# Ten record bodies instead of seven scattered after the attention's gathers, in a graph network kernel on one Trainium2 core

## The reference, cut to what matters

```python
edge_index = jnp.stack([src, dst])
x = x + attention(layernorm(x), edge_index)          # softmax over each node's edges, sum of att * h[dst]
x = x + token_ffn(layernorm(x))                      # router, top half of the tokens, 256 -> 1024 -> 256
x = x + gcn(layernorm(x), edge_index, type, attr)    # three layers over all edges
x = x + experts(layernorm(x))                        # two of 8 experts
...
ew = edge_attr @ edge_w + edge_b                     # inside gcn
msg = relu(x[src] * ew)
h_i = segment_sum(msg * (type == i), dst)            # for each of 3 types, then @ weights[l, i]
```

## Time and profile before

| | |
|---|---|
| three runs | 6016.11, 6029.7 and 6051.34 us, median 6029.7 us |
| the profiled execution | 6056.04 us, of it span 6054.2 us |
| busy in the span | PE 4511.0 us (75%), DVE 4198.5 (69%), POOL 4119.8 (68%), ACT 2286.1 (38%) |
| granted TensorE clock, mean | 0.895 |
| last sort step until the first gather of the attention | 1026 to 1114 us: PE busy 1.01 us, DVE 6.85, POOL 66.69 |
| attention | 1114 to 2181 us: PE busy 914.42 us, DVE 759.92, ACT 598.23, POOL 816.71 |
| token network | 2181 to 2414 us |
| three message layers | 2437 to 5780 us: POOL busy 819.51, 818.14 and 818.19 us in them |

### The profile page before, as it was taken

One profiled execution on the slowest core, in us unless ns is written; L12 is line 12 of the kernel. 1 busy time (PEld: TensorE's weight loads), 2 busy tenths in 40 slices (PEclk: granted clock), 3 DMA queues, 4 the chain that ended last, 5 costly groups with the idle time before them and its releaser, 6 DMA issues.

```text
span 6054.2 us, 89560 instructions
## 1 busy us (share of the span) xinstructions
PE 4511.0 (75%) x25082; PEld 2816.0 (47%) x25082; DVE 4198.5 (69%) x9658; ACT 2286.1 (38%) x5880; POOL 4119.8 (68%) x4199
## 2 busy tenths in 40 slices
PE   6469986488888879677777767777777677777787
PEld 2135543366666646344444434444444344444455
DVE  8889986377777773676666657767676677777734
ACT  0039875355555532333333323333332232323321
POOL 1467777777777774777777757777776777777700
PEclk9579998688888879899899989999999899999989
DMA  5011110234333321544444434444444444444400
GB/s 147 19 39 29 26 27 22 72 105 109 107 101 101 102 57 39 164 135 135 128 130 130 132 104 138 137 139 138 139 139 121 133 139 138 139 138 139 138 29 21
DMA packets 445004, 624.93 MB, mean 103 GB/s; under 512 B 97098, under 2 KB 330260, under 8 KB 444563
## 3 DMA queue, kind: packets, MB, share of 16 engines
q0 software_dynamic: 187648, 457.52, 27.2%
q1 hardware_dynamic: 250164, 159.14, 9.3%
q10 hardware_dynamic: 6754, 2.96, 0.2%
HBM read 556.32 MB, written 62.94 MB: 102 GB/s over the span
## 4 chain that ended last, share of the span: by engine, by line
PE 27%; DVE 15%; issue 10%; POOL 6%; ACT 2%; DVEq 2%; DMA 2%; SPq 0%; POOLq 0%; ACTq 0%
PE banks L1169 13%; DVE acc_mem L1688 6%; POOL sort_mem L619 6%; DVE z_mem L1831 5%; PE banks L1199 4%; PE banks L1112 3%; PE banks L1102 3%; DMA sort_mem<-x_d,x_mem 2%; PE banks L1157 2%; DVEq L1677 1%; DVEq L1688 1%; ACT z_mem L805 1%; PE banks L1154 1%; ACT x_mem L816 1%; PE banks L1189 1%
## 5 line engine op out<-in xcount | busy, mean ns | idle before, releaser
L619 POOL DMA_INDIRECT sort_mem<-x_d,x_mem x2568 | 2461.9, 959 | 953.1 <-issue 831.5
L1169 PE MATMUL banks<-z_mem 128*128 128x257 f32 x5136 | 1579.8, 432 | 907.0 <-DVE acc_mem L1688 773.1
L1169 PEld LDWEIGHTS banks<-z_mem 128*128 128x128 f32 x5136 | 858.1, 200 | 1605.7 <-ACT z_mem L805 717.6
L1688 DVE TENSOR_TENSOR acc_mem<-acc_mem,banks 128x257 f32 x2568 | 1080.2, 421 | 565.2 <-PE banks L1169 391.2
L805 ACT ACTIVATE z_mem<-z_mem 128x512 f32<-128x512 f32 x1284 | 768.8, 628 | 1381.1 <-DVE z_mem L1831 1381.1
L1831 DVE TENSOR_TENSOR z_mem<-banks,sort_mem 128x512 f32<-128x512 f32 x1284 | 825.1, 685 | 411.9 <-PE banks L1157 292.8
L577 POOL DMA_INDIRECT recB_d<-acc_mem,sort_mem x740 | 787.8, 1065 | 428.1 <-issue 223.0
L586 POOL DMA_INDIRECT acc_mem<-h_d,xnt_mem x808 | 803.6, 995 | 246.3 <-issue 230.2
L1045 PE MATMUL banks<-acc_mem,xnt_mem 128*128 128x257 f32 x1616 | 577.3, 484 | 43.3 <-DVE acc_mem L1631 42.2
L1631 DVE SCALAR_TENSOR_TENSOR acc_mem<-acc_mem,z_mem,banks 128x257 f32 x808 | 386.4, 478 | 115.5 <-PE banks L1045 98.8
L1157 PE MATMUL banks<-z_mem,x_mem 32*128 32x256 f32 x5136 | 422.6, 405 | 0.0
(11 more groups left out here) (347 smaller groups left out, 5663.9 us busy)
## 6 DMA issues: line engine op xcount, KB each, us to landing
x_mem<-recB_d SPq DMA_DIRECT2D x642, 68.0 KB
sort_mem<-x_d,x_mem POOLq DMA_INDIRECT x2568
x_mem<-at_d SPq DMA_DIRECT2D x428, 64.0 KB
at_d<-x_mem SPq DMA_DIRECT2D x214, 64.0 KB
acc_mem<-h_d,xnt_mem POOLq DMA_INDIRECT x808, 2.8
x_mem<-x_d SPq DMA_DIRECT2D x100, 128.0 KB, 2.7
acc_mem<-in_edge_attr SPq DMA_DIRECT2D x40, 312.5 KB
recB_d<-acc_mem,sort_mem POOLq DMA_INDIRECT x740, 2.2
```

The costliest lines, as they stand in the source:

```text
L619: pool.indirect_dma_start(out=xg[h % XG][:, k, :], out_offset=None, in_=x_ds[l % 2], in_offset=bass.IndirectOffsetOnAxis(ap=reci[h][:, k, ...
L1169: m.matmul(bank[5 + tile % 2][:, :AC], oneh[:, Q % 2, k, :], msg[:, Q % 2, k, :], start=True, stop=True)\
L1688: v.tensor_tensor(a_, a_, bank_[:, :AC], ALU.add).then_inc(flushed, 1)
```

## The change

`SCATTERED_FIRST` becomes 30, and a new name, `RANKED_BESIDE`, keeps the old 33 for all that concerns the ranks: late ranks, their bank, their steps and the steps at which records are made stay as they were. So bodies 30, 31 and 32 are ranked and their records made as before, but POOL scatters them after the attention's gathers. The four slots of the ring then hold bodies 30 to 33, and bodies 34 to 39 need a slot each: four lie in the sort's memory, which is laid out anew so that what sort A alone needs stands together, one in `z_mem`, one in a new tensor. Room for that comes from `winpA`, packed window numbers that nothing read, and its four DVE instructions go. The products of the router's weights move to `acc_mem` (`tok_dots`), and a small memset of DVE moves behind the wait for the scatters.

```diff
-SCATTERED_FIRST = RANKED_FIRST + PAIRS // 4
+RANKED_BESIDE = RANKED_FIRST + PAIRS // 4
+SCATTERED_FIRST = RANKED_BESIDE - 3
...
-        late_recs = [sort_mem[:, a:a + 20 * RW].rearrange("p (c w) -> p c w", w=RW) for a in (EC, EC + 20 * RW, 5 * EC)]
+        late_mem = [sort_mem[:, 7 * EC // 2 + k * 20 * RW:7 * EC // 2 + (k + 1) * 20 * RW] for k in range(4)]
+        late_mem += [z(1650, 20 * RW), sb("late_rec", [P, 20 * RW])]
+        late_recs = [m_.rearrange("p (c w) -> p c w", w=RW) for m_ in late_mem]
...
-            return bank[4 + g % 2 if g < 4 * SCATTERED_FIRST else 7][:EP, :5 * BKT_B]
+            return bank[4 + g % 2 if g < 4 * RANKED_BESIDE else 7][:EP, :5 * BKT_B]
...
-            return 3 + 3 * (g - 4 * SCATTERED_FIRST)
+            return 3 + 3 * (g - 4 * RANKED_BESIDE)
...
-                if i >= 4:
-                    act.wait_ge(S(f"edges_put{i % 4}"), i // 4 * 320 if i < SCATTERED_FIRST + 4 else (i - 4) // 4 * 320)
+                if 4 <= i < SCATTERED_FIRST + 4:
+                    act.wait_ge(S(f"edges_put{i % 4}"), i // 4 * 320)
...
-                for i in range(SCATTERED_FIRST, BODIES):
+                for i in range(RANKED_BESIDE, BODIES):
                     if s_ == record_step(i):
                         make_records(i)
...
-                st.did(v.scalar_tensor_tensor(s["winp"], four[:, :, 1], 128.0, four[:, :, 0], ALU.mult, ALU.add))
...
-                st.run(v.tensor_tensor(dots, xn[:, t0:t0 + 5, :], vecs[:, 0:1, :].broadcast_to([P, 5, D]), ALU.mult))
-                st.run(v.tensor_reduce(tok_w[:, t0:t0 + 5], dots, X_AXIS, ALU.add))
+                st.run(v.tensor_tensor(tok_dots, xn[:, t0:t0 + 5, :], vecs[:, 0:1, :].broadcast_to([P, 5, D]), ALU.mult))
+                st.run(v.tensor_reduce(tok_w[:, t0:t0 + 5], tok_dots, X_AXIS, ALU.add))
...
-            st.did(v.memset(msg[:, :, :, D:AC], 1.0))
             for u in range(4):
                 dve.wait_ge(S(f"edges_put{u}"), BODIES // 4 * 320)
+            st.did(v.memset(msg[:, :, :, D:AC], 1.0))
```

More of the change, by code:

```diff
@@ L144, in build @@
         sort_mem = sb("sort_mem", [P, 7 * EC])
[L145 to L150, removed]
+        keyB = sort_mem[:EP, 0:EC // 2].bitcast(BF16)
+        itemB = sort_mem[:EP, EC // 2:5 * EC // 2].rearrange("p (c e) -> p c e", c=2)
+        addrB = sort_mem[:, 5 * EC // 2:7 * EC // 2].bitcast(INT32)
+        keyA = sort_mem[:EP, 7 * EC // 2:4 * EC].bitcast(BF16)
+        dstm, segp, tileA = (sort_mem[:EP, (4 + k) * EC:(5 + k) * EC] for k in range(3))
+        winpB = sb("winpB", [1, TB // 4], INT32)
         ordp = sb("ordp", [1, 4 * NT], INT32)
@@ L264, in build @@
         xt = xt_mem[:, 0:2 * NP_].rearrange("p (k n) -> p k n", k=2)
+        tok_dots = acc_mem[:, 0:5 * D].rearrange("p (t d) -> p t d", d=D)
         tok_w = small[:, 330:355]
@@ L308, in build @@
         baseB_d, baseA_d = dram("baseB_d", [3, EC * BKT_B], BF16), dram("baseA_d", [3, EC * BKT_A], BF16)
-        SORT_B = dict(nb=BKT_B, T=TB, cols=5, bodies=EC // 20, key=keyB, base_d=baseB_d, winp=winpB, n=0)
-        SORT_A = dict(nb=BKT_A, T=TA, cols=10, bodies=EC // 40, key=keyA, base_d=baseA_d, winp=winpA, n=1)
+        SORT_B = dict(nb=BKT_B, T=TB, cols=5, bodies=EC // 20, key=keyB, base_d=baseB_d, n=0)
+        SORT_A = dict(nb=BKT_A, T=TA, cols=10, bodies=EC // 40, key=keyA, base_d=baseA_d, n=1)
         GROUPS_B, GROUPS_A = EC // 5, EC // 10
@@ L323, in late_bank @@
         def late_bank(g):
-            return bank[4 + g % 2 if g < 4 * SCATTERED_FIRST else 7][:EP, :5 * BKT_B]
+            return bank[4 + g % 2 if g < 4 * RANKED_BESIDE else 7][:EP, :5 * BKT_B]
         def record_slot(i):
             return erec[:, i % 4, :, :] if i < SCATTERED_FIRST + 4 else late_recs[i - SCATTERED_FIRST - 4]
-        assert BODIES - SCATTERED_FIRST <= 7
+        assert BODIES - SCATTERED_FIRST <= 4 + len(late_recs)
         def late_step(g):
-            return 3 + 3 * (g - 4 * SCATTERED_FIRST)
+            return 3 + 3 * (g - 4 * RANKED_BESIDE)
         def record_step(i):
-            return 5 + 10 * (i - SCATTERED_FIRST)
+            return 5 + 10 * (i - RANKED_BESIDE)
         block = ctx.enter_context(nc.Block())
@@ L560, in _ @@
             g.memset(tri_b, 1.0).then_inc(S("p_const"), 1)
-            pool.wait_ge(S("p_const"), 15)
+            pool.wait_ge(S("p_const"), 12 + len(late_recs))
             g.memset(pick[:, 79:80], 1.0).then_inc(S("p_const"), 1)
@@ L565, in _ @@
                    base=0, channel_multiplier=24).then_inc(S("p_const"), 1)
-            pool.wait_ge(S("p_const"), 18)
+            pool.wait_ge(S("p_const"), 15 + len(late_recs))
             pool.sem_inc(S("fill_ready"), 1)
@@ L654, in make_records @@
                 a.activation(rec_[:, :, W_SEG], itemB[:, 1, i * 20:(i + 1) * 20], ACT.Copy).then_inc(S("attr_hi"), 1)
-            act.wait_ge(S("p_const"), 17)
+            act.wait_ge(S("p_const"), 14 + len(late_recs))
             act.wait_ge(S("items_ready"), 1)
@@ L928, in rank_late @@
                 pe.wait_ge(S("onehot2"), g + 1)
-                if g >= 4 * SCATTERED_FIRST:
+                if g >= 4 * RANKED_BESIDE:
                     pe.wait_ge(S("maskedB"), g)
@@ L1067, in _ @@
                         sum_rows(s_ - 2, k)
-                for g in range(4 * SCATTERED_FIRST, 4 * BODIES):
+                for g in range(4 * RANKED_BESIDE, 4 * BODIES):
                     if s_ == late_step(g):
@@ L1239, in _ @@
             st = Steps(dve, "dve_step")
-            dve.wait_ge(S("p_const"), 17)
+            dve.wait_ge(S("p_const"), 14 + len(late_recs))
             st.did(v.tensor_scalar(ident, iota, iota_col, None, ALU.is_equal))
@@ L1352, in count @@
                 st.run(v.tensor_scalar(w[:, 512:T], bank[6][:, :T - 512], float(nb), None, ALU.min))
-                four = w[0:1, :T].rearrange("p (a b) -> p a b", b=4)
-                upper = winge[0:1, :T // 4].bitcast(INT32)
-                st.did(v.scalar_tensor_tensor(s["winp"], four[:, :, 1], 128.0, four[:, :, 0], ALU.mult, ALU.add))
-                st.run(v.scalar_tensor_tensor(upper, four[:, :, 3], 128.0, four[:, :, 2], ALU.mult, ALU.add))
-                st.run(v.tensor_single_scalar(upper, upper, 14, ALU.logical_shift_left))
-                st.run(v.tensor_tensor(s["winp"], s["winp"], upper, ALU.bitwise_or))
-                if n_ == 0:
+                if n_ == 0:
+                    four = w[0:1, :T].rearrange("p (a b) -> p a b", b=4)
+                    upper = winge[0:1, :T // 4].bitcast(INT32)
+                    st.did(v.scalar_tensor_tensor(winpB, four[:, :, 1], 128.0, four[:, :, 0], ALU.mult, ALU.add))
+                    st.run(v.scalar_tensor_tensor(upper, four[:, :, 3], 128.0, four[:, :, 2], ALU.mult, ALU.add))
+                    st.run(v.tensor_single_scalar(upper, upper, 14, ALU.logical_shift_left))
+                    st.run(v.tensor_tensor(winpB, winpB, upper, ALU.bitwise_or))
                     dve.wait_ge(S("order_pe"), 2)
@@ L1635, in _ @@
                 turns_, sums_ = 0 <= s_ - 1 < OCTS, 0 <= s_ - 2 < OCTS
-                late = [g for g in range(4 * SCATTERED_FIRST, 4 * BODIES) if s_ in (late_step(g), late_step(g) + 1)]
+                late = [g for g in range(4 * RANKED_BESIDE, 4 * BODIES) if s_ in (late_step(g), late_step(g) + 1)]
                 if s_ >= 3:
```

## The result

| | before | changed | ratio (95% interval) |
|---|---|---|---|
| first comparison, median | 6030.2 us | 5954.9 us (5950.9 to 5957.3) | 0.9862 (0.9847 to 0.9878) |
| second comparison, median | 6038.7 us | 5969.7 us (5960.7 to 5973.8) | 0.9886 (0.9867 to 0.9906) |
| profiled execution, span | 6054.2 us | 5949.1 us | |

The forecast was 5964 us, a gain of 66. The medians differ by 75.4 us in the first comparison and by 69.1 in the second. The ratios are not the plain quotients of these medians; by their intervals the gain is 74 to 92 us in the first comparison and 57 to 80 in the second.

What follows compares the result with a forecast made beforehand. POOL's gapless queue of indirect DMAs ahead of the attention's gathers was taken as the bound. Gains of 75.85 + 1.64 less 11.5 made 66 us, so 5964 us from the median 6029.7; range 5942 to 5994.

Steps and rivals of the forecast that it cites:

- The front, 75.85 us: Ahead of the attention: without sixty scatters POOL's first gather starts at 1037.86 instead of 1113.71, 75.85 us earlier.
- Rival 2: At the sorts' end: the gather list comes later, so the first gather misses 1037.86; 20 us lost gives 5984; chance 0.08.
- The margin of 12.9 us: Before the attention: the gather list, complete at 1024.99, is ready 12.9 us before the first gather's forecast start.
- `winpA`, 1.6 us: Ahead of the first ranks POOL waits for: four DVE instructions fewer save 1.6 us, lower bound 0.
- Sixty scatters at the back, 0.5 us dearer: Behind the gathers, beside DVE: 1.273 us each instead of 1.265; scatters land 15 us after the token network ends.
- rivals 1 and 4: POOL and DVE collide at the back: gain 40 to 58, chance 0.15; or 6.25 us per blocked scatter, slower, chance 0.02.
- The give-back, 11.5 us: At the message layers' start: scatters landing 15 us after the token network delay clearing and POOL's start, costing 11.5 us.
- The sum: Whole kernel: 75.85 + 1.64 - 11.5 = 66 us gained, 5964 us from the median.
- main case: Whole kernel: the forecast's own account holds, a gain of 58 to 72 us; chance 0.62.
- Rival 3, a gain of 77.5 us: In the message layers: they make up for their late start, nothing is given back, time 5952; chance 0.10.
- Rival 1: Last third of token network: collisions cost 11.8 us, or 1.343 us per scatter; gain 40 to 58, chance 0.15.

Runs made afterwards that it cites:

- layout_only: moved_0 with `winpA` and its four DVE instructions back; 6037.5 us, ratio 1.0006 to the kernel before.
- moved_0: The changed kernel with no body moved, all 33 scattered ahead of the gathers; 6029.2 us, ratio 0.9980 to the kernel before.
- before_plus_60: The kernel before with bodies 37 to 39 scattered a second time behind all scatters, and waited for; 6067.0 us, ratio 1.0020 to the kernel before.
- after_plus_60: The changed kernel with the last three bodies' 60 scatters repeated behind all others, and waited for; 6063.0 us, ratio 1.0008 to the kernel before.
- no_winp: The kernel before without the four DVE instructions on `winpA`, layout and scatters unchanged; 6032.2 us, ratio 0.9990 to the kernel before.
- before_again: The kernel before, unedited, run for a second profile; 6038.2 us, ratio 0.9988 to the kernel before.

## Why the prediction was right

*The front, 75.85 us.* Right. DVE's wait and POOL's queue changed as forecast: from the list to the first gather 88.7 us before, 11.6 and 12.9 now, so 77.1 and 75.8 less. Rival 2 fell: the gather starts behind a scatter, not behind the list. The margin of 12.9 us held, at 11.6 to 12.9 in all five profiles with three bodies moved, though their lists lie between 1005.4 and 1033.6 us: the list itself follows POOL, since ACT's records wait for bodies that POOL has scattered.

*`winpA`, 1.6 us.* Open. With the same layout, body 7's first scatter, which waits for DVE's ranks, starts 0.63 us earlier without the four instructions in one pair of profiles. POOL's timeline in layout_only, then in moved_0:

```profile
397.84 1.13 POOL L581 DMA_INDIRECT recB_d<-acc_mem,sort_mem  x1 [15.36 <-DVE sort_mem L1423]
```

```profile
397.21 1.13 POOL L581 DMA_INDIRECT recB_d<-acc_mem,sort_mem  x1 [15.36 <-DVE sort_mem L1423]
```

The old layout gives 0.71 (397.40 and 396.69). But the nine profiles without the four instructions have this start anywhere from 396.27 to 397.90 us, the five with them from 397.40 to 400.08, and the means are 1.4 us apart. So no pair sizes the term, and its worth in time is below what these runs can tell.

*Sixty scatters at the back, 0.5 us dearer.* They cost 76.0 us instead of 75.9: 0.1 us dearer, so DVE's additions do not hold POOL up here (11.8 us, had they done so), and rivals 1 and 4 fall. The last scatter started at 2326.22, not near 2350, only because sorts and attention ended earlier; its place against the token network is what the step rested on, and there it said 15 us, measured 14.1 to 15.4 until ACT's clearing begins.

*The give-back, 11.5 us.* Right in mechanism and size: the second multiplication is 11.0 and 12.3 us further behind the network's end, before_plus_60 shows 12.0, and 13.3 us in time. The first multiplication came 24.05 us after the clearing began, as forecast. POOL's own start was 9.1 us after the clearing began where 8.3 were forecast: the last store is issued at 2331.62 behind the feeds.

*The sum.* In the two profiles the parts that the change touches give -77.1 + 11.0 = -66.1 us. The other 39.0 us of the 105.1 are sorts (17.6), attention and token network (4.8) and the layers from the second multiplication on (16.6). Their instructions are the same but for the four and a few moved operands. Between the two profiles of the changed kernel the same stretches differ by 5.0, 4.9 and 9.8 us. The profiled execution of before was a long one on all of them, as its 26 us above the median had said; the changed kernel's has the shortest layers of all 14.

How near the total came is in part luck. The forecast's 66 us lie within the ratio's interval in the second comparison (57 to 80) and below it in the first (74 to 92), where the median's 75.4 is also above the 58 to 72 of its main case. From moved_0 to the changed kernel, the three bodies alone, the ratios fall by 0.0094 and 0.0118, 57 and 71 us, where the forecast had 64. What is left over in the first comparison may lie in the sorts, for which the forecast had 1.6 us and moved_0 allows 5 to 19; that is not shown.

*Rival 3, a gain of 77.5 us*, is nearer to the first median (75.4) than the forecast and farther from the second (69.1). The traces speak against it, since the give-back stands in each of them, and the 76 us of after_plus_60. The layers do not get shorter by starting late: from the second multiplication on they take 3594 to 3615 us in the nine profiles that start them 30 us behind the network's end (mean 3605), and 3594 to 3609 in the five that start them later (mean 3603), 3603.5 in after_plus_60 at 116.9 us. But a few microseconds that the layers take back would not be seen. Rival 1's own two prices gave gains of 55 and 62 us, and its range of 40 to 58 leaves out the second; nothing hangs on that.

## What to carry to other kernels

When a queue that runs without a gap stands ahead of a phase that everything waits for, and the same queue idles behind it, move work across until the idle time is used up: up to there each piece gains its length, 25.3 us for the first body here. Beyond it the queue's own end is awaited, and each scatter costs there what it takes, as after_plus_60 shows, so nothing more should be gained; no run moved a fourth body. The idle time shrinks by as much as the front gains, since the work that was awaited there comes earlier too. Before reading a difference of two profiles as the change's, compare stretches whose instructions did not change; here they held 39 of 105 us.

## What the runs showed of the hardware

Beside some sequences of DVE instructions a scatter of POOL is held up, and how many are held differs from one profile to the next. In a stretch of the old sorts, POOL's timeline and then DVE's:

```profile
657.59 2.54 POOL L577 DMA_INDIRECT recB_d<-acc_mem,sort_mem  x1 [0.30 <-issue]
660.43 2.11 POOL L577 DMA_INDIRECT recB_d<-acc_mem,sort_mem  x1 [0.30 <-issue]
```

```profile
657.97 0.68 DVE L1528 TENSOR_TENSOR acc_mem<-iota_b,acc_mem 125x512 f16<-125x512 bf16 x1
658.57 1.44 DVE L1532 TENSOR_SCALAR acc_mem<-acc_mem,sort_mem 125x808 f16<-125x808 f16 x4
```

The first scatter ends at 660.13, 0.12 us after the four comparisons of L1532 are done. In all 14 profiles every scatter of over 2 us between 300 and 990 us, 1 to 15 of them, ends 0.11 to 0.13 us after such a group. Between 640 and 680 us of this trace three are held so; the others, beside the same lines, take 0.96 to 1.20 us, one 1.89. What held the scatters of 1.4 to 2 us was not traced. In no_winp and before_again, whose scatters take 1034 and 1104 ns in the mean, the time above 0.96 us adds up to 37 and 67 us in that window, and 26 of the 31 us between them lie in scatters of over 1.4 us. POOL runs without a gap from body 9 on, so the end of the sorts moves with it: their lists are 34 us apart.

The scatter of 7.61 us in the changed kernel ends 0.8 us after L1699 (2092.85 against 2092.03). In all 14 profiles one scatter of 5.2 to 8.4 us ends 0.82 to 0.84 us after that sequence of 25 instructions, while the one to three that started earlier beside the same sequence took 0.95 to 1.28.

The Trainium skill, page "SBUF — State Buffer", section "SBUF: two separate sides", says that whichever of the two engines takes the shared ports first keeps them for the whole instruction. For L1528 with L1532, and for L1699, the trace agrees in that POOL goes on only when DVE is done. It does not show that the first to start wins: the scatter of 657.59 had started 0.38 us ahead of L1528, and other scatters ran on beside L1699; and POOL was held through several instructions in a row, not one. For the token network's additions, which read two operands from SBUF, no row shows a hold: the scatters beside them took 966 to 970 ns against 960.
